# Transformer layer on eight cores: load rings, first query angles and weight-mean pieces rearranged around attention

## The reference

```python
q = rope(x @ Wq.T + bq)             # 16 heads of 128
k = rope(x @ Wk.T + bk); v = x @ Wv.T + bv      # 4 KV heads, each for 4 query heads
attn = softmax(causal(q @ k.T / sqrt(128))) @ v
x = layernorm(x + attn @ Wo.T + bo)
# BitNet feed-forward, 2048 -> 8192 -> 2048
quant_act(x):    s = max(max|row|, 1e-5) / 127;  clip(round(x / s), -128, 127) * s
quant_weight(w): s = mean|w| + 1e-5;             clip(round(w / s), -1, 1) * s
h = sigmoid(quant_act(x) @ quant_weight(w_gate).T) * (quant_act(x) @ quant_weight(w_up).T)
x = layernorm(x + quant_act(h) @ quant_weight(w_down).T)
```

## Time and profile before

| | us |
|---|---|
| runs shown (three) | 2321.49, 2323.8, 2588.58; median 2323.8 |
| profiled execution | 2324.98 |
| its span on core 7, the slowest | 2323.4 |
| spans of the eight cores | 2302.0 to 2323.4 |
| TensorE busy | 2126.9 (92%) |
| VectorE busy | 1253.3 (54%) |
| ScalarE busy | 1205.1 (52%) |
| GpSimd busy | 363.8 (16%) |
| DMA | 603.18 MB, mean 260 GB/s |

### The profile page before, as it was taken

How to read it: one execution, slowest core, us unless ns; L and a number is a source line. 1 busy time by engine, 2 the same in 40 slices (tenths; PEclk the granted TensorE clock), 3 DMA queues, 4 the chain that set the end, 5 groups by cost and what they waited for, 6 DMA issues and landing times.

```text
span 2323.4 us, 34473 instructions; the slowest of 8 cores (2302.0 to 2323.4 us)
## 1 busy us (share of the span) xinstructions
PE 2126.9 (92%) x11420; PEld 1022.1 (44%) x11420; DVE 1253.3 (54%) x1746; ACT 1205.1 (52%) x1279; POOL 363.8 (16%) x329
## 2 busy tenths in 40 slices
PE   4989879798898888999999999999999987999995
PEld 1434334365565444444444444444444433444442
DVE  2657679877777477444444444444444765121213
ACT  1455335698898454555555555555343565323223
POOL 6656763011100122000000000000000002010010
PEclk9999989899999999999999999999999999999998
DMA  8999878799999665888988889888666699665584
GB/s 264 293 301 285 254 247 232 235 312 288 287 281 267 208 220 216 266 292 292 306 284 290 289 291 303 288 289 271 225 233 239 200 316 307 218 180 196 186 290 145
DMA packets 144620, 603.18 MB, mean 260 GB/s; under 512 B 16704, under 2 KB 16832, under 8 KB 109504
## 3 DMA queue, kind: packets, MB, share of 16 engines
q1 hardware_dynamic: 113040, 446.83, 59.9%
q10 hardware_dynamic: 24192, 121.65, 15.6%
q0 software_dynamic: 7216, 32.51, 4.6%
HBM read 544.29 MB, written 56.62 MB: 259 GB/s over the span
## 4 chain that ended last, share of the span: by engine, by line
PE 57%; DMA 13%; DVE 8%; ACT 8%; issue 6%; POOL 5%; ACTq 0%; SPq 0%; DVEq 0%; POOLq 0%
PE ps L659 19%; PE ps L674 18%; PE ps L713 14%; ACT PT L1131 6%; DMA stg<-xk 6%; DMA hld<-hd 4%; PE ps L568 2%; PE ps L550 2%; POOL XB L1310 1%; DMA stg<-xqt 1%; DVE h L937 1%; DVE asum L822 1%; DVE x1s L873 1%; DMA bo_b<-bo 1%; PE ps L528 1%
## 5 line engine op out<-in xcount | busy, mean ns | idle before, releaser
L659 PE MATMUL ps<-XT,WB 128*128 128x512 bf16 x2048 | 465.4, 380 | 5.7 <-DVE x1s L844 5.7
L674 PE MATMUL ps<-XT,WB 128*128 128x512 bf16 x2048 | 462.9, 379 | 0.0
L713 PE MATMUL ps<-DBR,HQT 128*128 128x512 bf16 x1536 | 332.2, 379 | 3.4 <-DVE x1r L1012 3.4
L1131 ACT ACTIVATE PT<-ps,negc 128x1024 bf16<-128x1024 f32 x288 | 295.2, 1113 | 35.3 <-PE ps L550 34.6
L659 PEld LDWEIGHTS ps<-XT,WB 128*128 128x128 bf16 x2048 | 201.0, 98 | 248.4 <-issue 9.2
L674 PEld LDWEIGHTS ps<-XT,WB 128*128 128x128 bf16 x2048 | 200.4, 98 | 241.4
L1234 ACT ACTIVATE sg<-gs 128x512 f32<-128x512 f32 x128 | 80.7, 630 | 391.5 <-DVE gs L970 391.5
L1206 ACT ACTIVATE dst<-dst,wrs 128x2048 int16<-128x2048 f32 x64 | 128.0, 2000 | 270.4 <-DMA dst<-wd 270.4
L970 DVE TENSOR_TENSOR gs<-ps,sgx_b 128x512 f32<-128x512 f32 x128 | 88.4, 691 | 313.6 <-PE ps L659 313.6
L1139 ACT ACTIVATE WST<-WST,wrs 128x2048 int16<-128x2048 f32 x128 | 254.0, 1988 | 0.0
L713 PEld LDWEIGHTS ps<-DBR,HQT 128*128 128x128 bf16 x1536 | 149.9, 98 | 185.7 <-issue 5.9
(11 more groups left out here) (158 smaller groups left out, 2392.8 us busy)
## 6 DMA issues: line engine op xcount, KB each, us to landing
WST<-wg SPq DMA_DIRECT2D x64, 1024.0 KB, 7.1
WST<-wu SPq DMA_DIRECT2D x64, 1024.0 KB, 7.7
wdm<-wd ACTq DMA_DIRECT2D x64, 1024.0 KB, 9.5
dst<-wd SPq DMA_DIRECT2D x53, 1024.0 KB, 5.9
stg<-xk SPq DMA_DIRECT2D x64, 512.0 KB, 13.8
hd<-hw SPq DMA_DIRECT2D x128, 256.0 KB, 8.5
hld<-hd SPq DMA_DIRECT2D x128, 256.0 KB, 7.8
MR<-wg ACTq DMA_DIRECT2D x60, 512.0 KB, 19.0
```

What stands on the lines that cost most here:

```text
L659: mm = te.matmul(ps[:, gb, :], WB[n % 6][:, 0, j, :], XT[:, j, hf * 512:(hf + 1) * 512], start=(j == 0), stop=(j == 15))
L674: mm = te.matmul(ps[:, ub, :], WB[n % 6][:, 1, j, :], XT[:, j, hf * 512:(hf + 1) * 512], start=(j == 0), stop=(j == 15))
L713: mm = te.matmul(ps[:, i, :], HQT[m][:, i * 128:(i + 1) * 128], DB(16 * c + mg)[:, k, :], start=(m == 0), stop=(m == 63))
L1131: a.activation(PT[u % 5][:, :, :, :].rearrange("p b h q -> p (b h q)"), ps[:, 2 * (u % 2):2 * (u % 2) + 2, :].rearrange("p b n -> p (b n)" ...
```

## The change

Five edits:

1. **Numbers of pieces.** K and V sum 52 pieces of |w| in place of 60, Q still 24, attention 158 in place of 152, and the projection 22 in place of 20. In K and V ScalarE does nine per block in place of ten, and one in the last block in place of four. In the projection the two additional ones stand in tile 4.
2. **First query angles.** GpSimd only makes the iota of `table(8)`, and VectorE the other seven instructions, after its unit 29. ScalarE's sine and cosine move behind unit 31.
3. **Ring.** Four slots `WS` are added in the upper half of `WKV[1]`, free once the third head group's Q matmuls are done (`pe_k` 56). They take the places after slots 0 and 1 and end one by one before `WO` needs the space. Slots 0 and 1 wait only for the casts, 2 and 3 for group A, and 4 to 11 for all of Q. The last pair of `KS` leaves the ring, and the other four end at piece 146, so the last 12 pieces have four slots.
4. **End of attention.** SP loads the bias rows and the first two residual tiles directly behind the ring, each when its space is free, and then the first five pieces of group C, which ScalarE loaded before. `attended` comes one unit earlier in VectorE's order.
5. **Means.** The sum of the partial means, its matmul and the scales move from tile 4 to tile 5. TensorE does the small matmul after chunk 1 in place of after the tile. SP issues the second and third gate/up weights after tile 4 in place of 3.

```diff
-NMEAN_KV = 60
-NMEAN_A = 84
-NMEAN_C = 20
+NMEAN_KV = 52
+NMEAN_A = 76
+NMEAN_C = 22
...
-B_FROM = [0] * 12 + [NMEAN_B * (g + 1) // 4 + 14 for g in (0, 0, 1, 1, 2, 2)]
-B_UNTIL = [NMEAN_B] * 4 + [NMEAN_B * (19 + 2 * x) // 33 - 16 for x in range(8)] + [NMEAN_B] * 6
+B_FROM = [0] * 12 + [NMEAN_B * (g + 1) // 4 + 14 for g in (0, 0, 1, 1)] + [0] * 4
+B_UNTIL = [NMEAN_B] * 4 + [NMEAN_B * (19 + 2 * x) // 33 - 16 for x in range(8)]
+B_UNTIL += [NMEAN_B - 12] * 4 + [NMEAN_B * (11 + 2 * x) // 33 - 16 for x in range(4)]
...
+_order = [0, 1, 16, 17, 18, 19, 2, 3, 4, 5, 6, 7, 8, 9, 10, 11, 12, 13, 14, 15]
+_last = [_order.index(k) - 40 for k in range(20)]
...
-MR_DONE = [max(n for n in range(NMEAN_B) if B_SLOT[n] == 4 + x) + 1 for x in range(8)]
+B_DONE = [_last[k] + 1 for k in range(20)]
...
+    WS = [sb("WS%d" % i, [128, 1024], F32, 122.5 + 4 * i) for i in range(4)]
...
         for n in range(NMEAN_B):
             k = B_SLOT[n]
-            if n == 0:
-                s.wait_ge(cast, 128)
-                s.wait_ge(mean_a, NMEAN_A)
-            if n == 4:
-                s.wait_ge(pe_k, 64)
             if B_PREV[n] >= 0:
                 s.wait_ge(mean_b, B_PREV[n] + 1)
-            elif k >= 12:
+            elif k < 2:
+                s.wait_ge(cast, 128)
+            elif k < 4:
+                s.wait_ge(mean_a, NMEAN_A)
+            elif k < 12:
+                s.wait_ge(pe_k, 64)
+            elif k < 16:
                 s.wait_ge(pe_s, 72 * ((k - 12) // 2 + 1))
+            else:
+                s.wait_ge(pe_k, 56)
...
-        s.wait_ge(pe_s, NU)
-        s.wait_ge(mean_b, NMEAN_B)
+        s.wait_ge(pe_s, 216)
+        s.dma_start(bo_b[:, :], bo.broadcast_to([128, 2048])).then_inc(bol, 16)
         for i in range(2):
+            s.wait_ge(mean_b, max(B_DONE[12 + 2 * i], B_DONE[13 + 2 * i]))
             s.dma_start(x1s[i][:, :], xq[i * 128:(i + 1) * 128, :]).then_inc(xrl[i], 16)
-        s.dma_start(bo_b[:, :], bo.broadcast_to([128, 2048])).then_inc(bol, 16)
+        for k in range(5):
+            if k < 2:
+                s.wait_ge(mean_b, B_DONE[k])
+            if k == 2:
+                s.wait_ge(cast_wo, 31)
+            if k == 3:
+                s.wait_ge(pe_s, NU)
+            s.dma_start((stg[1], stg[2], stg[0], KS[6], KS[7])[k][:, :],
+                        mean_src(NMEAN_A + NMEAN_B + k)).then_inc(mld[k], 16)
...
-            if i == 3:
+            if i == 4:
                 s.wait_ge(mean_a, NMEAN_A + NMEAN_C)
                 w_load(1)
                 w_load(2)
...
-            if i == 4:
-                te.wait_ge(ws_rdy, 1)
-                te.matmul(ps[:, 7, 0:2], onesf[:, :], wsum[:, 0:2], start=True, stop=True) \
-                    .then_inc(pe_ws, 1)
+                if i == 5 and c == 1:
+                    te.wait_ge(ws_rdy, 1)
+                    te.matmul(ps[:, 7, 0:2], onesf[:, :], wsum[:, 0:2], start=True, stop=True) \
+                        .then_inc(pe_ws, 1)
...
+            if i == 29:
+
+                v.wait_ge(iota0, 2)
+                done(v.tensor_scalar(tab_u[:, :], tab_u[:, :], cst_s[:, 2:3], invf[:, :],
+                                     OP.add, OP.mult))
+                done(v.tensor_scalar(tab_u[:, :], tab_u[:, :], 1.0 / (2.0 * math.pi), None, OP.mult))
+                reduced()
...
-        attend_at = {LAST_UNIT[tl] + 6 + min(3, (tl + 1) % 8 + 1): tl for tl in range(32)}
+        attend_at = {LAST_UNIT[tl] + 5 + min(3, (tl + 1) % 8 + 1): tl for tl in range(32)}
...
-                               (2, 2, 0, 0) if t == 7 else (2, 3, 2, 3))[m]):
+                               (1, 0, 0, 0) if t == 7 else (2, 2, 3, 2))[m]):
...
-                if t == 7 and m == 2:
+                if t == 7 and m == 3:
                     table(8)
...
-        a.wait_ge(pe_s, NU)
-        a.wait_ge(mean_b, NMEAN_B)
-        a.wait_ge(cast_wo, 32)
-        for k in range(5):
-            mean_load(NMEAN_A + k)
...
-            for k in range(4):
+            for k in range(4 if i < 4 else 2):
...
-        table(8)
+        g.wait_ge(tab_rd, 16)
+        g.iota(tab_u[:, :], [[512, 4], [1, 128]], base=0, channel_multiplier=0,
+               allow_small_or_imprecise_dtypes=True).then_inc(iota0, 1)
...
-            if w >= 16 and w % 2 == 0:
-                g.wait_ge(mean_b, MR_DONE[w // 2 - 8])
+            if w >= 8 and w % 2 == 0:
+                g.wait_ge(mean_b, B_DONE[w // 2 - 4 if w >= 16 else w // 2 + 12])
```

33 lines of the change are left out of this document (17 added, 16 removed).

## The result

The changed kernel takes 2300.4 us (median of 2299.45, 2300.38 and 2300.62) where the kernel before takes 2323.8 beside it (2321.49, 2323.8, 2324.24). The ratio is 0.9901 with a 95% interval of 0.9885 to 0.9916. The change gains 23 us of the 44 forecast, and the time is just outside the range (2263 to 2300). In some executions of both kernels and of several variants the cores of one die or of both ran at a lower granted clock than usual and the time was longer; these are left out of all times and ratios, and of the profile of `e8_small_loads`, which is such an execution, only cores 0 to 3 are read, whose clock was not lowered.

What follows compares the result with a forecast made beforehand. It took K and V as DMA-bound, with waits at attention's head-group changes and a late residual in the projection. Gains of 22 before attention, 9 in attention and 13 in projection made 44: 2324.98 to 2281, 2280 against the runs' median, range 2263 to 2300.

Steps and rivals of the forecast that it cites:

- The stage is bound by the DMA, with TensorE close under it: K and V blocks: 9.44 MB at 295 GB/s is 32 us for a 31.2 us block, DMA share 0.97.
- the 12 that I took: K and V: gain in us for GpSimd's casts from eight fewer pieces, between bounds of 8 and 16.2.
- rival B: K and V blocks keep their pace, set by ScalarE and VectorE; only the table's gain before Q; 2292, chance 0.17.
- step (b): Before Q: GpSimd's 12.05 us between two groups of casts become an iota of 0.57; 9 less, bounds 0 and 11.5.
- VectorE falls some 5 us behind, and I hide these under the wait of unit 36 for `table(9)`: Early Q: VectorE's table delays it 5 us, covered by a later wait; up to 5 if that cover is gone.
- The ring's tail: End of attention: loads for pieces 150 to 157 come late with short distances; cost 4 us, between 0 and 6.
- the 1 us a turn: Attention, changes of head group: half the half-clock slowing of matmuls after TensorE's stall goes, 1 us each.
- Without it I get 3.4 at the end: Projection: TensorE's 5.01 wait in tile 4 for the sum of the means goes, gaining 3.4 us.
- the early residual: Start of projection: bias and residual loaded sooner bring the first normalising to 800.5 from 809.92, 9.4 us less.
- Rival A: Attention: the DMA can't keep the ring fed, VectorE's waits delay masks and `attended`, attention gains nothing; 2289, chance 0.17.
- C: End of attention: the new tail blocks SP's in-order queue; at 252 GB/s attention takes 373 us; 2333, chance 0.04.
- D: The DMA relief is worth all of its bound, 25 + 17 + 18 = 60; 2265, chance 0.12.

Runs made afterwards that it cites:

- e8_small_loads: Changed kernel with 44 of K and V's pieces of |w| loaded to only 64 of 1024 columns, sums covering old contents; 2297.95 us in the one comparable run.
- b0_before: The kernel before the change, unchanged, profiled again on the chip of the later variants; 2315.0 us in its one run.
- e1_pieces_kv: Changed kernel with the eight pieces of |w| put back into K and V, attention's ring 150 in place of 158; ratio 0.9936 to the kernel before.
- e9_short_sums: Changed kernel with ScalarE summing only 64 of each piece's 1024 columns in K and V, all loads kept; ratio 0.9903 to the kernel before.
- e5_table_early: Changed kernel with the iota ahead of the casts of the first x tile and VectorE's table two units earlier; ratio 0.9903 to the kernel before.
- e10_c_spread: Changed kernel with five pieces behind each of projection tiles 0 and 1, none behind tile 4; ratio 0.9917 to the kernel before.
- e3_means_late: Changed kernel with the means' small matmul behind tile 4's transposes and the scales behind tile 5; ratio 0.9892 to the kernel before.
- e4_seam_back: Changed kernel with residual, bias and first loads of group C as before the change, after attention; ratio 0.993 to the kernel before.
- e6_attend_back: Changed kernel with `attended` one unit later again in VectorE's order; ratio 0.997 to the kernel before.

## Why the prediction was wrong where it was

**K, V and Q: 22 forecast, 6 to 12 measured. The step that failed is "The stage is bound by the DMA, with TensorE close under it".** It was argued from a share of 0.97 and from volume over rate, 32 us for 31.2. What TensorE waited for in these blocks I did not read there. The kernel before, core 7, TensorE's groups from 63 to 250 (last column: idle before, and what ended it):

```profile
L512 PE MATMUL ps<-WKV,XB 128*128 128x512 bf16 x384 | 88.3, 383 | 2.1 <-DVE VX L761 2.1
L501 PE MATMUL ps<-XB,WKV 128*128 128x512 bf16 x384 | 84.0, 379 | 0.2 <-POOL XB L1310 0.2
L518 PE MATMUL ps<-sq,ones 128*128 128x512 bf16 x24 | 9.3, 387 | 10.4 <-ACT sq L1086 9.5 <-DVE kmx L764 1.0
```

For its inputs TensorE waited 0.2 us in 187. All else were squares of ScalarE and copies of VectorE. The DMA feeds ScalarE's pieces of |w| as well, and on this core ScalarE did wait for them, in the same stretch:

```profile
ACT MR L1061 <- DMA MR<-wg: 25.8, 13, 5.8
```

So a part of the waits for squares may go back to the DMA in that execution. It can't carry the 12 that I took. ScalarE's waits for pieces in the six blocks are 1.9 in the changed kernel run again, 7.3 in `b0_before` and 19.2 in `e1_pieces_kv` (medians of the cores), and the blocks take 182.3, 182.6 and 184.7, the last among variants with fewer pieces that have up to 185.2. `e8_small_loads` shows it from the other side: 21.6 MB less, and the blocks are no faster. The equality of 32 and 31.2 was a coincidence. The Trainium skill (Perfetto Trace Analysis, "Identifying the Most-Contended Engine") warns that the occupancy of 16 DMA engines misleads, and ("Optimization Strategy") asks what ends the gaps of the engine in question. This case agrees with both: at a DMA share of 0.97, 0.2 us of TensorE's gaps ended with its inputs. My rival B said that the blocks keep their pace, because ScalarE and VectorE set it. That they keep it was right, and the chance of 0.17 was too low. The reason is right for the waits only: of 30.4 a block, 28.5 are TensorE's own matmuls, and `e9_short_sums` shows that behind ScalarE's squares the inputs come close. B's 2292 was too low as well, as it kept the 13 of the projection.

What fewer pieces did give was GpSimd's casts of Q's inputs, 8 us earlier (270.1 to 262.0). My step (b) had the hole right: the casts of the first query weights end 13.0 to 13.5 after those of the first half of `XQ` (14.2 forecast), where it was 22.3 to 22.6 before, and in all they end 14.4 to 18.5 earlier, 21 forecast. But then TensorE has only just come to the end of K and V, whose blocks are hardly faster, so Q starts 12.7 to 17 earlier. The second error lies behind it: "VectorE falls some 5 us behind, and I hide these under the wait of unit 36 for `table(9)`". They are not hidden. VectorE has K/V's last two rotations and then Q's behind the table, and their products mostly take 1.34 to 1.43 beside GpSimd's casts where they take 0.69 alone. Some 5 of the hole's gain go there (4.3 to 5.6 from Q's start to the first scores), and `e5_table_early` gets three or four of them back.

**Baseline: the profile read was one execution on one chip.** Run again on another, the kernel before has its first scores at 430.7 and not at 437.3. Its six blocks are 3.5 shorter there, so that much of the waits that I took as waste belonged to that execution or its chip (TensorE waits 8.4 in these blocks by the median, and 12.5 in the profile that I read).

**Attention: 9 forecast, 10 to 12 measured.** `attended` alone gives 11.3, 13 forecast. The ring's tail was to cost 4. Its waits are there, 7.9 in all on core 7, but with `attended` put back attention is as long as before, so tail and additional pieces together cost about nothing. At the first turn TensorE still waits 3.31, and the slow stretch behind it stays: 6.8 us at a granted clock of 0.50, before and after. At the second turn of core 7 it fell from 10.2 to 3.4, at the third it stays at 6.8. So the 1 us a turn for that was earned at one turn at most. That the forecast of attention came so near is in part luck, since the two terms were off in opposite directions. (A slip without consequence: the exponentials of the earlier trace rows are 1.014 apart by (43.70 - 1.11) / 42, not 1.005, which makes 292 of the 290.)

**Projection: 13 forecast, 1.3 to 2.3 measured. The step that failed is "Without it I get 3.4 at the end".** It counted what the sum's wait cost in its old place, and not what it would cost in its new one. That the two new pieces "fit, as tile 4 had none" is true of ScalarE's time, but the sum waits for them too (2 to 3 us by `e10_c_spread`). Above all the sum stands on VectorE behind tile 4's normalising, which was 5.18 long on core 7, while TensorE asks for it already after chunk 1 of tile 5. By the medians tile 5's normalising follows tile 4's by 24.9, before by 16.2: the lead of 7 to 8 that tile 4 still had is gone at tile 5. At the end of the projection 1 to 2 are left, where I had reckoned with the lead and 3.4 on top. The rest was a size: the early residual gives 6.4 to the first normalising (26.5 to 20.1), not 9.4. I took core 7, where it came 29.4 after the start, and the median of the cores is 26.5. `e3_means_late` confirms the reading from the other side: without the wait the projection takes 133.8, 5.6 less than before.

**Feed-forward: 0 forecast, 4 to 5 measured.** Every variant has 1392 to 1395 here, the kernel before 1396.8 and 1399.7, so a part may be the executions. Neither `e4_seam_back` nor `e6_attend_back` brings it back to that. Its cause stays open. Of the 23 gained, these 4 to 5 are luck as far as my account goes.

**The sum.** From the two later executions it is 6 + 12 + 2 + 4 = 24 of 44; the mean of the cores has 21.7 there and 24.2 on the first chip. Rival A didn't happen: the ring kept up at 324 GB/s but for its tail. C didn't happen either. D was the mistake carried further. (Its 2265 is counted from the profiled 2324.98, the others' times from the median of the runs.)

## What to carry to other kernels

A DMA share near one and a volume that divides to just the stage's time don't make a stage DMA-bound. Read what the bounding engine's idle time was ended by, and follow it to the engine behind: here TensorE waited 0.2 us in 187 for its inputs, and ScalarE's waits for pieces could grow from 2 to 19 without a visible effect on the blocks. And look which wait comes next: with ScalarE relieved, half of the cores waited for their inputs. Work that is taken off one engine should go into the other's idle time, and not between the last work of one stage and the first of the next; here that choice was worth 4 us of the table's 10. When a wait is moved, cost it in its new place, by what stands ahead of it in its producer's order: TensorE's wait for the sum of the means was 5 before and 8 (median) after, and behind tile 5 it was 0.5 or nothing.
